# Moving a layer norm's roots off GpSimd: square roots on ScalarE, reciprocals and offsets on VectorE

## The chip, the cores and the metric

One core of one Trainium2 chip runs the whole program in one launch. The metric is device time in microseconds (us). A core has TensorE (PE; its weight loads are PEld), VectorE (DVE), ScalarE (ACT), GpSimd (POOL) and SyncE (SP), each with a queue of its own that it works off in order; they wait for each other through semaphores.

## The reference

Eight layers follow each other, each with a residual and a layer norm behind it. The change lies in the seventh, an attention over learned keys (4096 keys of 128, values of 128), on x of shape 4 x 1024 x 128:

```python
Q = jnp.einsum('bsd,bdr->bsr', x, shared_compress)
scores = jnp.einsum('bsr,nr->bsn', Q, K) / math.sqrt(K.shape[1])
topk_scores, topk_idx = jax.lax.top_k(scores, 8)
weights = jax.nn.softmax(topk_scores, axis=-1)
selected_V = V[topk_idx]
output = jnp.einsum('bskd,bsk->bsd', selected_V, weights)
...
r = x + output
x = (r - mean(r)) / jnp.sqrt(var(r) + 1e-5)
```

## The kernel before

The stage is `top_keys_stage`. A prelude works out `shared_compress`; after it the stage runs over 32 tiles of 128 tokens (ALL = 32), eight to a batch, in eight groups of four (PER_HALF = 4, GROUPS = 8). All of it is written out straight, with no hardware loop, and the order on each engine is that of the calls in its function. For tile t:

- TensorE multiplies the queries of the tile by all 4096 keys, in four chunks of 1024 columns (L2945), into two banks that ScalarE must empty by turns. Behind the chunks of tile t it mixes tile t - 6 (`mix`, L2931): eight products with the identity add the eight weighted values.
- ScalarE copies the chunks to `scores` (L2619), of which four tiles are kept. Between the second and the third chunk it weights the gathered values of tile t - 6 (`scale`, eight instructions, L2596), before the fourth it normalises tile t - 14 (`normalise`, L2606). Behind the last chunk comes `weigh` for tile t - 1: it waits for the eight best scores, negates the largest (L2585) and takes the exponentials (L2587). Behind the loop it works off what is left: `scale` up to tile 31, and `normalise` up to tile 31, one tile of each a turn.
- VectorE searches the eight best scores of tile t (`dve.max`, L2746) and their indices (L2748), then closes tile t - 5 (`close`): reciprocal of the sum of weights, r = mix * inverse + x (L2760), and mean and variance into `moments` (L2763, L2764). `close` waits for the mix of its tile.
- GpSimd gathers the values of tile t (`gather`): eight indirect DMAs (L2534), one for each of the eight indices; they wait for the indices of tile t and for the mix of tile t - 8, whose slot they use. `root(g)` stands behind `gather(4g + 8)`: it waits for the moments of the four tiles of group g, and then takes four operations of 128x4, among them (var + eps) to the power -0.5 (L2525, L240, L241, L2527). They give `rstd` and `offset` = -mean * rstd, by which `normalise` computes y = r * rstd + offset on ScalarE.
- SP stores y a group at a time (L2498, it waits for `normalise` of the group's last tile), loads x again for the groups to come (L2494), and behind the store of the group before the last fetches the first input of the next stage (`next_x`, L2506). The stage ends when the last stores have landed.

The next stage, `routed_experts_stage`, begins with a transpose of that input, and its first exponential on ScalarE is L3112.

## Time and profile before

| | us |
|---|---|
| median of three runs | 2123.44 (2122.04 to 2123.99) |
| profiled execution, its own time | 2122.32 |
| its span | 2120.4 |
| TensorE busy in the span | 1879.8 (89%) |
| VectorE busy | 1569.4 (74%) |
| ScalarE busy | 1227.2 (58%) |
| GpSimd busy | 610.6 (29%) |
| gathers of the stage (L2534), 256 | 242.3, mean 947 ns |
| root operations on GpSimd, 4 x 8 | 13.2 |

The stage with the gathers takes the span from about 1510 to 1977 us; its loop over tiles begins near 1608. The shares of busy time are means over stages with different limits, so they don't say what bounds this one; the timelines of the stage do. A timeline row gives the start and the length in us, engine, line, operation, output and inputs, and in square brackets how long the engine had stood idle before it and what ended that ("issue": nothing that the profile shows). Issue rows of SP and GpSimd are the issuing of a DMA, not the transfer.

### The profile page before, as it was taken

The numbers are of one execution on the slowest core, as the hardware profiler recorded it, in microseconds if no ns is written. First come the engines' busy times: TensorE is split into PE (matmuls) and PEld (weight loads), VectorE is DVE, ScalarE is ACT, GpSimd is POOL, SyncE is SP. The second block draws the span as 40 slices with busy tenths as digits, with TensorE's granted clock in tenths as the row PEclk, the third lists the DMA queues.
The fourth block names the chain that finished last, engine by engine and source line by source line (L and its number), as shares of the span: only waits on it lengthen the run. The fifth ranks groups of instructions, "written<-read, shape, count | busy, mean of one in ns | idle before, by whom it ended". The sixth has DMA issues, their size and how long they took to land. (4 is left out here: it accounts for less than half of the span.)

```text
span 2120.4 us, 31998 instructions
## 1 busy us (share of the span) xinstructions
PE 1879.8 (89%) x10615; PEld 1279.2 (60%) x10624; DVE 1569.4 (74%) x3770; ACT 1227.2 (58%) x2532; POOL 610.6 (29%) x801
## 2 busy tenths in 40 slices
PE   7999979999699999579999999999789989983797
PEld 5667644444477777458888887888664444443342
DVE  4555547677448888658999999999435999994498
ACT  3334436666255555178888887887214667673465
POOL 2221216778302121200000000000002777777122
PEclk9999989999699999789999999999779999996799
DMA  2000020000300000000000000000400122222100
GB/s 91 30 30 0 30 87 11 16 6 11 104 6 11 21 11 11 10 15 2 6 16 6 2 16 6 1 6 16 190 2 14 53 56 61 69 61 61 45 26 25
DMA packets 34695, 65.80 MB, mean 31 GB/s; under 512 B 8406, under 2 KB 19742, under 8 KB 33782
## 3 DMA queue, kind: packets, MB, share of 16 engines
q1 hardware_dynamic: 26358, 47.16, 6.5%
q0 software_dynamic: 8192, 16.79, 3.1%
q8 instruction: 80, 1.31, 0.3%
q14 instruction: 65, 0.53, 0.1%
HBM read 51.34 MB, written 12.58 MB: 30 GB/s over the span
## 5 line engine op out<-in xcount | busy, mean ns | idle before, releaser
L2183 DVE SCALAR_TENSOR_TENSOR pk_level<-pk_sums,pk_least 128x1024 f32<-128x1024 f32 x256 | 321.7, 1276 | 22.9 <-ACT pk_sums L2092 21.6
L2092 ACT ACTIVATE pk_sums<-pk_sum 128x512 f32<-128x512 f32 x512 | 278.7, 602 | 94.5 <-PE pk_sum L2302 92.1
L2534 POOL DMA_INDIRECT tk_values<-top_keys_values,tk_index x256 | 242.3, 947 | 196.4 <-DVE tk_index L2748 118.4
L2310 PE MATMUL pk_weights<-product_keys_early_ident,pk_level 128*128 128x128 f32 x2048 | 269.5, 274 | 26.3 <-DVE pk_level L2183 24.3
L2310 PEld LDWEIGHTS pk_weights<-product_keys_early_ident,pk_level 128*128 128x128 f32 x2048 | 225.9, 141 | 52.9 <-DVE pk_level L2183 33.8
L2945 PE MATMUL tk_to_act<-tk_keys,tk_xT 128*128 128x512 f32 x512 | 233.0, 602 | 23.2 <-ACT tk_scores L2619 22.1
L2945 PEld LDWEIGHTS tk_to_act<-tk_keys,tk_xT 128*128 128x128 f32 x512 | 94.1, 192 | 144.3 <-issue 92.5
L1755 PEld LDWEIGHTS er_outs<-experts_early_w,er_hT 128*128 128x128 f32 x1024 | 134.0, 192 | 59.7 <-issue 56.4
L1165 PE MATMUL ml_outs<-experts_early_we,ml_xT 128*128 128x512 f32 x320 | 161.3, 632 | 3.5 <-DVE ml_r L1022 3.5
L2302 PE MATMUL pk_sum<-pk_lay_corners,pk_partsT 96*128 96x256 bf16 x1024 | 154.2, 272 | 0.9 <-ACT pk_sums L2092 0.9
L2746 DVE MAX8 tk_best<-tk_scores 128x8 f32<-128x4096 f32 x32 | 141.1, 4409 | 15.1 <-ACT tk_scores L2619 15.1
L240 POOL TENSOR_TENSOR pk_plus_eps<-pk_moments,pk_eps 128x4 f32<-128x4 f32 x8 | 11.2, 1406 | 452.3 <-DVE pk_moments L224 452.3
L2748 DVE FIND_INDEX8 tk_index<-tk_best,tk_scores 128x8 uint32<-128x4096 f32 x32 | 141.4, 4419 | 0.0
L1022 DVE SCALAR_TENSOR_TENSOR ml_r<-ml_outs,ml_gates,ml_r 128x128 f32<-128x128 f32 x384 | 105.0, 342 | 47.7 <-PE ml_outs L1165 36.7
L1448 ACT ACTIVATE er_hT<-er_to_act,experts_early_b 128x512 f32<-128x512 f32 x128 | 85.5, 686 | 93.2 <-PE er_to_act L1744 92.3
L2619 ACT ACTIVATE tk_scores<-tk_to_act 128x1024 f32<-128x1024 f32 x128 | 126.2, 1011 | 20.4 <-PE tk_to_act L2945 20.4
L1755 PE MATMUL er_outs<-experts_early_w,er_hT 128*128 128x128 f32 x1024 | 134.5, 275 | 0.0
L1744 PE MATMUL er_to_act<-er_xT,experts_early_w 128*128 128x512 f32 x256 | 133.4, 604 | 0.0
L2073 ACT ACTIVATE pk_partsT<-pk_to_act 96x1024 bf16<-96x1024 bf16 x128 | 132.0, 1036 | 0.0
L2302 PEld LDWEIGHTS pk_sum<-pk_lay_corners,pk_partsT 96*128 96x128 bf16 x1024 | 99.6, 97 | 26.0 <-issue 15.4
L2931 PE MATMUL tk_to_dve<-tk_values,top_keys_early_ident 128*128 128x128 f32 x512 | 69.6, 295 | 38.6 <-ACT tk_values L2596 38.6
L891 ACT ACTIVATE ml_scaled<-ml_outs,ml_gates 128x128 f32<-128x128 f32 x256 | 70.1, 387 | 52.7 <-PE ml_outs L1165 51.6
(437 smaller groups left out, 3677.4 us busy)
## 6 DMA issues: line engine op xcount, KB each, us to landing
tk_scores<-top_keys_compress SPq DMA_DIRECT2D x1, 4096.0 KB
tk_values<-top_keys_values,tk_index POOLq DMA_INDIRECT x256, 2.5
att_x_proj<-x_first SPq DMA_DIRECT2D x4, 512.0 KB, 5.0
att_x_res<-x_first SPq DMA_DIRECT2D x4, 512.0 KB, 4.3
x_after_attention<-att_y SPq DMA_DIRECT2D x4, 512.0 KB, 4.9
experts_early_w<-experts_w SPq DMA_DIRECT2D x2, 1024.0 KB
x_after_attention<-ml_y SPq DMA_DIRECT2D x8, 256.0 KB, 2.0
experts_ahead_x<-x_after_attention SPq DMA_DIRECT2D x8, 256.0 KB, 3.3
```

The source lines that it names most:

```text
L1165: pe.matmul(outs[f % len(outs)][:], xT[:, b % 2, t * P:(t + 1) * P], we[:, n * PER_FILL:(n + 1) * PER_FILL, :].rearrange("p e d -> p (e d) ...
L1744: pe.matmul(bank[:], w1[:, n, :], xT[:, t % 2, :], start=True, stop=True).then_inc(A.full.sem, 1)
L1755: ins = pe.matmul(bank[:, s * P:(s + 1) * P], hT[:, (t * CHUNKS + n) % (LAG + 1), s * P:(s + 1) * P], w2[:, n, :], start=k == 0 and s == 0 ...
L2073: act.activation(partsT[:, t % 3, s * PER_FILL:(s + 1) * PER_FILL, :].rearrange("k n p -> k (n p)"), bank[:].bitcast(BF16)[0:STACK, 0:PER_ ...
L2092: act.activation(sums[:, n % SUMS, half * HALF:(half + 1) * HALF], bank[:], ACT.Copy).then_inc(S.free.sem, 1)
L2183: dve.scalar_tensor_tensor(level[:, n % LEVELS, :], sums[:, n % SUMS, :], least[:, t % 2, h:h + 1], sums[:, n % SUMS, :], ALU.is_ge, ALU.m ...
L2302: ins = pe.matmul(by_column[:, j], partsT[:, t % 3, h * FILLS + c, :], lay_corners[:, c], start=True, stop=True)
L2310: ins = pe.matmul(weights[:, ch * P:(ch + 1) * P], level[:, n % LEVELS, ch * P:(ch + 1) * P], ident[:], is_transpose=True, start=h == 0 an ...
L2534: pool.indirect_dma_start(out=values[:, slot, k, :], out_offset=None, in_=c["values"], in_offset=bass.IndirectOffsetOnAxis(ap=index[slot][ ...
L2746: dve.max(best[:, slot, :], scores[:, t % KEPT, :]).then_inc(best_ready, 1)
L2748: dve.max_index(index[slot][:], best[:, slot, :], scores[:, t % KEPT, :]).then_inc(index_ready, 1)
L2945: ins = pe.matmul(bank[:, half * HALF:(half + 1) * HALF], xT[:, b, at * P:(at + 1) * P], keys[:, first:first + HALF], start=True, stop=True)
```

## The change

The four root operations leave GpSimd. `deviate(g)` on ScalarE takes the square root of var + eps for the four tiles of group g; in the loop it stands behind the last chunk of tile 4g + 10 and ahead of `weigh`, and for groups 6 and 7 in the turns 34 and 38 behind the loop, ahead of `normalise` of that turn (tiles 20 and 24). `offset_of(g)` on VectorE takes the reciprocal and -mean * rstd; it stands behind the close of tile 4g + 5, and for the last group at the very end. GpSimd's queue then holds the gathers alone, and three of its constants go.

```diff
+    ROOT_LAG = 2 * PER_HALF + 2
...
-            pool.memset(power[:], -0.5).then_inc(built, 1)
             pool.memset(eps[:], LN_EPS).then_inc(built, 1)
-            pool.memset(minus_one[:], -1.0).then_inc(built, 1)
-            pool.wait_ge(built, 4)
-
-            def root(g):
-
-                group = half_of(g)
-                pool.wait_ge(moments_ready, (g + 1) * PER_HALF)
-                after(pool, offset_ready, g)
-                steps.do(pool.tensor_tensor(minus_mean[:], moments[:, group, 0], minus_one[:], ALU.mult))
-                steps.link(rsqrt_on_pool(steps, pool, rstd[:, group], moments[:, group, 1], plus_eps[:], eps[:], power[:]))
-                pool.tensor_tensor(offset[:, group], minus_mean[:], rstd[:, group], ALU.mult).then_inc(offset_ready, 1)
+            pool.wait_ge(built, 2)
...
-            for t in range(ALL + CLOSE_LAG):
-                if t < ALL:
-                    gather(t)
-                g, at = divmod(t - CLOSE_LAG, PER_HALF)
-                if g >= 0 and at == PER_HALF - 1:
-                    root(g)
+            for t in range(ALL):
+                gather(t)
...
+            def deviate(g):
+
+                group = half_of(g)
+                act.wait_ge(moments_ready, (g + 1) * PER_HALF)
+                act.activation(deviation[:, group], moments[:, group, 1], ACT.Sqrt, bias=eps[:]).then_inc(deviation_ready, 1)
...
+                if t >= ROOT_LAG and (t - ROOT_LAG) % PER_HALF == 0:
+                    deviate((t - ROOT_LAG) // PER_HALF)
                 if t >= 1:
                     weigh(t - 1)
...
+                if t >= ROOT_LAG and (t - ROOT_LAG) % PER_HALF == 0 and (t - ROOT_LAG) // PER_HALF < GROUPS:
+                    deviate((t - ROOT_LAG) // PER_HALF)
                 normalise(t - NORM_LAG)
...
+            def offset_of(g):
+
+                group = half_of(g)
+                dve.wait_ge(deviation_ready, g + 1)
+                after(dve, y_ready, (g - 1) * PER_HALF)
+                steps.link(dve.reciprocal(rstd[:, group], deviation[:, group]))
+                dve.scalar_tensor_tensor(offset[:, group], moments[:, group, 0], -1.0, rstd[:, group],
+                                         ALU.mult, ALU.mult).then_inc(offset_ready, 1)
...
                 if t >= CLOSE_LAG:
                     close(t - CLOSE_LAG)
+                    g, at = divmod(t - CLOSE_LAG, PER_HALF)
+                    if at == 1 and g >= 1:
+                        offset_of(g - 1)
...
+            offset_of(GROUPS - 1)
```

## Rows read from the trace of the kernel before

**Rows 1.** Source view and timeline of the gathers: ns min/median/max, range; then start, length

```profile
L2534 POOL DMA_INDIRECT tk_values<-top_keys_values,tk_index x256: 940/944/1209, 1628.5 to 1959.5; - x128
...
1628.50 1.21 POOL L2534 DMA_INDIRECT tk_values<-top_keys_values,tk_index  x1 [117.44 <-DVE tk_index L2748]
```

**Rows 2.** Timeline, GpSimd (POOL), around its sixth root and its last gather

```profile
1927.50 0.95 POOL L2534 DMA_INDIRECT tk_values<-top_keys_values,tk_index  x1 [0.30 <-issue]
...
1928.47 0.21 POOL L2525 TENSOR_TENSOR tk_minus_mean<-tk_moments,tk_minus_one 128x4 f32<-128x4 f32 x1
...
1930.73 1.02 POOL L2534 DMA_INDIRECT tk_values<-top_keys_values,tk_index  x1 [0.51 <-issue]
...
1932.06 0.94 POOL L2534 DMA_INDIRECT tk_values<-top_keys_values,tk_index  x1 [0.30 <-issue]
...
1959.51 0.94 POOL L2534 DMA_INDIRECT tk_values<-top_keys_values,tk_index  x1 [0.30 <-issue]
```

**Rows 3.** Timeline, VectorE (DVE): index searches of tiles 8 and 31

```profile
1697.03 4.42 DVE L2748 FIND_INDEX8 tk_index<-tk_best,tk_scores 128x8 uint32<-128x4096 f32 x1
...
1923.75 4.42 DVE L2748 FIND_INDEX8 tk_index<-tk_best,tk_scores 128x8 uint32<-128x4096 f32 x1
```

**Rows 4.** Timeline of one tile in the steady part, ScalarE (ACT) and TensorE (PE)

```profile
1801.50 1.01 ACT L2619 ACTIVATE tk_scores<-tk_to_act 128x1024 f32<-128x1024 f32 x1
...
1805.38 0.20 ACT L2585 ACTIVATE tk_minus<-tk_best 128x1 f32<-128x1 f32 x1 [2.87 <-DVE tk_best L2746]
...
1805.62 0.30 ACT L2587 ACTIVATE tk_weight<-tk_best,tk_minus 128x8 f32<-128x8 f32 x1
...
1806.97 3.70 PE L2945 MATMUL tk_to_act<-tk_keys,tk_xT 128*128 128x512 f32 x8 [0.92 <-ACT tk_scores L2619]
```

**Rows 5.** Timeline, ScalarE, table loads of an earlier stage

```profile
591.30 1.28 ACT L1452 ACT_TABLE_LOAD   x1
...
592.60 0.21 ACT L1452 ACTIVATE er_exps<-er_shifted 128x16 f32<-128x16 f32 x1
...
632.53 1.28 ACT L1470 ACT_TABLE_LOAD   x1
...
635.81 0.42 ACT L1470 ACTIVATE er_probs<-er_biased 128x256 f32<-128x256 f32 x1 [2.00 <-DVE er_biased L1600]
```

**Rows 6.** Groups of instructions: busy us, mean ns; a reciprocal of 128x4

```profile
L2725 DVE RECIPROCAL tk_neuron_sum<-tk_neuron_sum 128x4 f32<-128x4 f32 x1 | 0.2, 178 | 0.0
```

**Rows 7.** Timeline, end of the stage

```profile
1964.42 2.02 ACT L2606 ACTIVATE tk_y<-tk_r,tk_offset,tk_rstd 128x128 f32<-128x128 f32 x5
...
1964.92 1.86 SPq L2498 DMA_DIRECT2D x_after_top_keys<-tk_y  x2
...
1969.31 0.18 DVE L2764 BATCH_NORM_AGGREGATE tk_moments<-tk_stats 128x2 f32<-128x6 f32 x1
...
1971.31 1.65 ACT L2606 ACTIVATE tk_y<-tk_r,tk_offset,tk_rstd 128x128 f32<-128x128 f32 x4 [4.87 <-POOL tk_offset L2527]
...
1972.98 0.32 SPq L2498 DMA_DIRECT2D x_after_top_keys<-tk_y  x1
...
1977.73 0.10 POOL L3073 MEMSET moe_power<- 128x4 f32 x1 [6.45 <-POOLq L154]
```

**Rows 8.** DMA issues at the stage's end: count, KB each, us from issue to landing

```profile
x_after_top_keys<-tk_y SPq DMA_DIRECT2D x3, 256.0 KB, 2.0
...
experts_ahead_x<-x_after_top_keys SPq DMA_DIRECT2D x1, 512.0 KB, 3.5
```

**Rows 9.** Timeline, ScalarE, first exponential of the next stage

```profile
1984.16 0.22 ACT L3112 ACTIVATE moe_expo<-moe_gate_bank 128x64 f32<-128x64 f32 x1 [3.67 <-PE moe_gate_bank L3268]
```

**Rows 10.** Windows: length, busy us by engine, TensorE clock granted, DMA share, GB/s

```profile
1700.00:1800.00 100.00, 90.62 (x325) 48.12 (x324) 98.61 (x72) 69.30 (x162) 75.97 (x85) 1.00 0.22 59
...
856.30:858.96 2.66, 0.01 (x2) 0.01 (x1) 2.66 (x2) 0.00 (x0) 0.00 (x0) 1.00 0.00 0
...
863.82:866.00 2.18, 1.44 (x5) 0.92 (x6) 1.80 (x9) 1.47 (x2) 1.47 (x2) 0.74 0.00 0
```

More of the change, by code:

```diff
@@ L2395, in top_keys_stage @@
         ones = m.sb("ones", [P, P])
-        power = m.sb("power", [P, PER_HALF]); eps = m.sb("eps", [P, PER_HALF]); plus_eps = m.sb("plus_eps", [P, PER_HALF])
-        minus_one = m.sb("minus_one", [P, PER_HALF]); minus_mean = m.sb("minus_mean", [P, PER_HALF])
+        eps = m.sb("eps", [P, 1]); deviation = m.sb("deviation", [P, KEPT_R])
         x = first_x.x; xT = m.sb("xT", [P, B, T])
@@ L2444, in top_keys_stage @@
         gathered = [m.sem(f"gathered{i}") for i in range(SLOTS)]
-        r_ready, moments_ready, offset_ready, y_ready = (m.sem(n) for n in ("r_ready", "moments_ready", "offset_ready", "y_ready"))
+        r_ready, moments_ready, deviation_ready, offset_ready, y_ready = (
+            m.sem(n) for n in ("r_ready", "moments_ready", "deviation_ready", "offset_ready", "y_ready"))
         dve_steps, pool_steps = m.sem("dve_steps"), m.sem("pool_steps")
@@ L2885, in _ @@
             ins.then_inc(chain_full, 1)
-            pe.wait_ge(built, 4)
+            pe.wait_ge(built, 2)
             pe.wait_ge(chain_ready, 4)
```

## The prediction

> **What bounds the kernel now.** I read the views in this order: the page's list of groups, to find the stage (it runs from about 1510 to 1977 us of the span); the source view of the gathers; the timeline of each engine in the steady part; then the timeline of the stage's end. The question at each is who is never idle.
>
> GpSimd is. Its 256 gathers begin at 1628.50, after one wait of 117.44 us for the first index, and the last begins at 1959.51 [rows 1]. In an undisturbed stretch they start (1959.51 - 1932.06) / 22 = 1.248 us apart: about 0.94 of work and 0.30 of issue. Where a root stands between two gathers, the starts 1927.50 and 1932.06 are 4.56 us apart and not 2.50, so one root costs the queue 2.06 us [rows 2]. Of the eight roots six stand between gathers; in GpSimd's loop root(g) follows gather(4g + 8), and only g = 0 to 5 are followed by more gathers. The sum closes: 255 x 1.248 + 0.27 for the longer first gather + 6 x 2.06 = 330.8 us, against 331.0 measured [rows 1, 2]. So GpSimd waits for nobody after its start, and its queue alone sets the time of the last gather.
>
> VectorE is the close second. From tile 8 to tile 31 its index searches start (1923.75 - 1697.03) / 23 = 9.86 us apart [rows 3]; GpSimd needs 8 x 1.248 = 9.98 us a tile without roots. ScalarE has 2.87 us of every tile to spare, in which it waits for the best scores, and TensorE waits 0.92 us once a tile for a bank that ScalarE must empty [rows 4].
>
> **The roots leave GpSimd.** 6 x 2.06 = 12.4 us go out of the queue that sets the end. Root 6 and root 7 stand behind the last gather and belong to the tail, below. The last gather then starts at 1959.51 - 12.4 = 1947.1, if the index is there. What is late next? Index 8 is ready at 1697.03 + 4.42 = 1701.5, and gather 8 would start at 1628.8 + 64 x 1.248 = 1708.6: 7.2 us of reserve. Index 31 is ready at 1928.2, gather 31 would start at 1628.8 + 248 x 1.248 = 1938.3: 10.1 us [rows 1 to 3]. The reserve pays for what VectorE gets.
>
> **VectorE takes a reciprocal and a product per group.** Six of the eight offset_of calls come before the index of tile 31. A reciprocal of 128x4 took 0.18 us [rows 6]; a product of the same size I take alike, and two gaps of 0.04: 0.43 us each call, 2.6 us in all, from a reserve of 10.1. Between 0.36 (no gaps) and 1 us a call this costs nothing. It does not wait either: offset_of(g) stands after tile 4g + 10, and its deviation is made by ScalarE behind the scores of tile 4g + 10, a tile before VectorE searches that tile. If it did wait, the next max search would be queued behind it, and behind that the indices of all later gathers.
>
> **ScalarE takes eight square roots, and table loads with them.** The steady part has only copies, exponentials and identities, and no load. In an earlier stage, where Gelu and Exp alternate, each change shows a load of 1.28 us, and the activation starts 0.02 us behind it (591.30 + 1.28, then 592.60) [rows 5]. The load does not wait for the data of its activation: at 632.53 it runs at once, and the activation follows at 635.81 after 2.00 us of waiting for VectorE [rows 5]. In the loop deviate(g) stands between the last scores of a tile and weigh. The load for Sqrt and the root itself (0.21 us for an exponential of 128x16 [rows 5], 0.30 for one with a bias read from memory [rows 4]; I take 0.30) need 1.6 us and fall into the 2.87 us of waiting. The moments are two tiles old by then, so no wait is added. The load back to Exp falls behind minus, after the best scores have come: 1.3 us, six times, in which the scores of the next tile are not taken and TensorE waits 2.2 us instead of 0.92. TensorE works 90.62 of 100 us at full clock, 8.93 us a tile, so it wins back 0.92 us a tile, 3.7 us in a group of four [rows 4, 10]. ScalarE itself has 4 x 2.87 = 11.5 us a group for 2.9 us of additions. Cost: nothing, with TensorE's spare time as the cover; without it, up to 6 x 1.3 = 7.8 us.
>
> The Trainium skill speaks against this part. "ScalarE: Activation LUTs", section "What ACT_TABLE_LOAD costs", gives 2.66 us for a change of set, with a drain, and the section on table sets says to do all of one set before the other. By its figure, 13 changes would be an estimate of 35 us of ScalarE and not 17, but the sum would stay, since 5.6 us a group still fit in 11.5; the trace shows 1.28 and no gap for a drain [rows 5]. The figure would lengthen TensorE's stops to some 3.6 us, which bears on the last rival.
>
> **The next stage.** It starts with an exponential, and the set is now that of Sqrt. ScalarE stands idle 3.67 us before it [rows 9], and by rows 5 the load runs before the wait: nothing. If the load came behind the wait: 1.28 us on the way to the gates. I take nothing.
>
> **The tail.** The last moments come at 1969.31 + 0.18 = 1969.49. Now the root on GpSimd ends and ScalarE normalises the last four tiles from 1971.31 to 1972.96: 3.47 us behind the moments [rows 7]. The four tiles of group 6 were normalised at 1964.42 (five in 2.02 us) while the last tile was still in work [rows 7]. After the change deviate(7) stands before them in ScalarE's queue and waits for the last moments. So behind the moments come a hop of 0.03, the root 0.30, and eight tiles at 0.40 to 0.41: 3.6 us; VectorE's offset (0.43) is hidden behind the first four. That is 0.1 us worse (0 to 0.4). No second load is due there, since root 6 has left the set in place.
>
> Moved with these tiles are DMAs on SP's queue: the store of group 6, and behind it the fetch of the next stage's first input, both of which used to be issued before the last moments [rows 7]. They are now issued some 2.0 to 2.6 us behind the moments, and the last store at 3.6. The fetch takes 3.5 us to land and a store 2.0 [rows 8]. If the last store shares the engines with the fetch, it starts late: it lands at 5.6 undisturbed, and at 2.6 + 3.5 + 2.0 = 8.1 if all of it follows the fetch. Between 0 and 2.5 us; I take 1.1, since only its data and not its start-up has to follow. From the last store's issue to the next stage 1977.73 - 1972.98 = 4.75 us pass as before [rows 7].
>
> **The sum.** -12.4 + 0.1 + 1.1 = -11.2 us. The profiled execution took 2122.32 us (span 2120.4), so it would become 2111.1 (span 2109.2). The median of the three runs is 1.1 above the profiled one; on the median I forecast 2112. The bounds: -12.4 gives 2111.0; tail at its worst (+2.9), 2114; with 1.28 for the next stage's load, 2115.2. Medians spread by about 1 us.
>
> **Rivals.** (A) VectorE becomes the bound. It happens if an offset_of costs more than 10.1 / 6 = 1.7 us, say because it waits for ScalarE. At 2.87 us each, the length of ScalarE's own wait, index 31 comes at 1928.2 + 17.2 = 1945.4, 7.1 behind the queue: 2119. For it: VectorE has 98.61 us busy in 100 [rows 10], no spare time at all. Against it: the deviation is ready a tile ahead.
>
> (B) The tail costs far more: the late fetch and stores pile up by more than their landing times say, or the next stage's load is exposed too: 2116.
>
> (C) The change does not shorten the queue: what follows a root is not the root but something that the ring of gathers needs anyway, so that gathers stretch by what the roots free. Time 2123. Against it: 22 gathers in a row keep 1.248 us [rows 2], and the DMA engines are at 0.22 [rows 10].
>
> (D) Slower: TensorE's clock. The six stops of 2.2 us let the granted clock fall, and TensorE, which has 0.92 us of spare time a tile, becomes the bound. After a single stop of 2.66 us in an earlier stage the clock was still 1.00 (from 856.30), but in the stretch from 863.82, after a second stop close behind, 0.74 [rows 10]. If a whole tile then ran at half clock, a group would lose 8.9 + 1.3 - 3.7 = 6.5 us; six are 39 us. Two covers come off once. GpSimd's reserve of 10.1 less the 2.6 for VectorE is 7.5 us. The scores of a tile, done at 1801.50 + 1.01, are there 8.3 us before their max search: the search before ends at 1805.38, so theirs starts at 1805.38 + 9.86 - 4.42 = 1810.8 [rows 3, 4]. 39 - 15.8 - 11.2 = 12 us slower than before: 2135. It decides from a loss of (15.8 + 11.2) / 6 = 4.5 us a group; below that the kernel is still faster. Against it: one stop of 2.2 us in 39 us of work is less than what left the clock at 1.00. The stops of 3.6 us by the Trainium skill's figure would make it likelier.
>
> **Chances.** Forecast (2109.5 to 2115) 0.78; A 0.05; B 0.08; C 0.04; D 0.05. The range 2109 to 2117 takes in the forecast and B. A measurement of this kernel tells 0.2% (4.2 us) from no change: faster means below 2119.2. Forecast, B and half of A are faster: 0.89; C and the other half 0.06; slower is D, 0.05.
>
> **What would show it.** Right: GpSimd's line has only gathers, from about 1628.5 to 1947.1, always 1.248 apart; seven loads for Sqrt and six for Exp in ScalarE's lines, of 1.28 us, and one more in the next stage before its wait; TensorE's waits of 0.92 become 2.2 once a group and its clock stays at 1.00; MAX8 never waits for scores; the last three DMA issues of the stage lie within 2 us. Wrong: waits of gathers for tk_index (A), gathers longer than 1.248 apart (C), a clock below 1.00 between 1700 and 1900 (D), a stage whose end lies more than 10 us behind the last moments (B). The forecast also falls if the loads do not run ahead of waits.

## The result, and the profile after

The changed kernel took 2110.3 us (median of four runs, 2108.26 to 2111.31) against 2123.53 (2122.04 to 2123.99) for the kernel before on the same chip: a ratio of 0.9935, 95% interval 0.992 to 0.995. That is faster by 13.2 us; the forecast was 11.2 us less and 2112 for the median, with a range from 2109 to 2117. The profiled execution took 2110.27, its span is 2108.4.

The page of the changed kernel, span and busy time of each engine (share of the span, instructions):

```profile
span 2108.4 us, 32001 instructions
...
PE 1884.2 (89%) x10615; PEld 1281.7 (61%) x10624; DVE 1571.8 (75%) x3786; ACT 1249.2 (59%) x2554; POOL 597.4 (28%) x767
```

Busy shares have hardly moved. TensorE is busy a little longer than before (1884.2 against 1879.8) and the kernel is 12 us shorter. The page doesn't say where they went; the source view of the gathers, now line 2524, does (ns min/median/max, first and last start, then the idle time before them):

```profile
L2524 POOL DMA_INDIRECT tk_values<-top_keys_values,tk_index x256: 940/944/1212, 1631.2 to 1949.8; - x128
...
  DVE tk_index L2744: 119.4, 1
  issue: 76.8, 252
  PE tk_to_dve L2940: 0.9, 3
```

256 gathers now run from 1631.2 to 1949.8, 318.6 us, against 331.0 in [rows 1]. They wait for an index once, at the start. So the 12.4 us are gone and nothing has moved into their place. To find the rest, both spans were cut at the same events, all read from timelines. The differences add up to the -12.0 us of the spans:

| stretch of the span, us | before | after | difference |
|---|---|---|---|
| stages before this one | 1510.92 | 1511.83 | +0.91 |
| start of the stage to first gather | 117.58 | 119.41 | +1.83 |
| first gather to last gather | 331.01 | 318.59 | -12.42 |
| last gather to last moments | 9.98 | 10.00 | +0.02 |
| last moments to end of the last y | 3.47 | 3.40 | -0.07 |
| last y to issue of last store | 0.02 | 0.03 | +0.01 |
| issue of last store to next stage | 4.75 | 4.65 | -0.10 |
| the last stage | 142.68 | 140.46 | -2.22 |

The third row is the change. The second and the last are larger than any change of the tail, and were not in the forecast.

One group boundary in the steady part of the changed kernel, ScalarE and TensorE by the timeline; it answers to [rows 4]:

```profile
1786.15 1.28 ACT L2590 ACT_TABLE_LOAD   x1
1787.45 0.30 ACT L2590 ACTIVATE tk_deviation<-tk_moments,tk_eps 128x4 f32<-128x4 f32 x1
1789.00 0.20 ACT L2571 ACTIVATE tk_minus<-tk_best 128x1 f32<-128x1 f32 x1 [1.25 <-DVE tk_best L2742]
1789.22 1.28 ACT L2573 ACT_TABLE_LOAD   x1
1790.52 0.30 ACT L2573 ACTIVATE tk_weight<-tk_best,tk_minus 128x8 f32<-128x8 f32 x1
1791.87 5.40 PE L2954 MATMUL tk_to_act<-tk_keys,tk_xT 128*128 128x512 f32 x8 [2.21 <-ACT tk_scores L2611]
```

ScalarE loads its table at once and takes the root, all within what was an idle time of 2.87 us; 1.25 us of it are left before `minus`. Then comes the load back, after the best scores are there, and the exponential of `weigh` and the next copy of scores are 1.3 us later than they were. TensorE stops for 2.21 us instead of 0.92. Six stops of 2.21 us stand in the loop. Behind three of them the eight matmuls took 5.40 us and not 3.70. TensorE's timeline, then windows (length, busy us by engine, granted clock, DMA share, GB/s):

```profile
1712.42 5.40 PE L2954 MATMUL tk_to_act<-tk_keys,tk_xT 128*128 128x512 f32 x8 [2.21 <-ACT tk_scores L2611]
1752.10 3.70 PE L2954 MATMUL tk_to_act<-tk_keys,tk_xT 128*128 128x512 f32 x8 [2.21 <-ACT tk_scores L2611]
...
1710.00:1720.00 10.00, 7.79 (x27) 4.32 (x27) 9.86 (x8) 8.10 (x18) 7.55 (x8) 0.83 0.19 53
1750.00:1760.00 10.00, 7.90 (x31) 4.55 (x32) 9.86 (x8) 8.36 (x20) 7.54 (x8) 1.00 0.21 54
1790.00:1800.00 10.00, 8.13 (x27) 4.58 (x28) 9.86 (x8) 8.07 (x19) 7.54 (x8) 0.83 0.20 52
```

The windows behind the stops of 1712.42 and 1791.87 have a granted clock of 0.83 (part of them at the lower of its two levels, 1.2 GHz), the one behind 1752.10 has 1.00. VectorE, in its timeline, does what it was given, and its max searches wait for scores only once, before the first:

```profile
1923.42 0.16 DVE L2767 RECIPROCAL tk_rstd<-tk_deviation 128x4 f32<-128x4 f32 x1
1923.62 0.20 DVE L2768 SCALAR_TENSOR_TENSOR tk_offset<-tk_moments,tk_rstd 128x4 f32<-128x4 f32 x1
```

### The profile page after: what moved, and what is told of

The parts are those of the page before. It is cut to its first block and busy times, and to the rows that moved or that the text cites. A ratio compares the mean times of both kernels' runs of the same rounds, so it can differ in the third digit from the quotient of the medians.

```text
span 2108.4 us, 32001 instructions
## 1 busy us (share of the span) xinstructions
PE 1884.2 (89%) x10615; PEld 1281.7 (61%) x10624; DVE 1571.8 (75%) x3786; ACT 1249.2 (59%) x2554; POOL 597.4 (28%) x767
## 5 line engine op out<-in xcount | busy, mean ns | idle before, releaser
L2524 POOL DMA_INDIRECT tk_values<-top_keys_values,tk_index x256 | 241.8, 945 | 197.1 <-DVE tk_index L2744 119.4
L240 POOL TENSOR_TENSOR pk_plus_eps<-pk_moments,pk_eps 128x4 f32<-128x4 f32 x8 | 11.2, 1406 | 453.1 <-DVE pk_moments L224 453.1
L1165 PEld LDWEIGHTS ml_outs<-experts_early_we,ml_xT 128*128 128x128 f32 x320 | 59.7, 200 | 63.4 <-issue 51.9
```

Of the source, the lines that this page charges most:

```text
L1165: pe.matmul(outs[f % len(outs)][:], xT[:, b % 2, t * P:(t + 1) * P], we[:, n * PER_FILL:(n + 1) * PER_FILL, :].rearrange("p e d -> p (e d) ...
L2524: pool.indirect_dma_start(out=values[:, slot, k, :], out_offset=None, in_=c["values"], in_offset=bass.IndirectOffsetOnAxis(ap=index[slot][ ...
```

## The experiments

All are edits of the changed kernel but for "roots twice", an edit of the kernel before. A figure for the gathers is the start of the last less the start of the first. The theory: the roots' time in GpSimd's queue is the whole gain, and what was added to ScalarE and VectorE is hidden. The rivals are those of the prediction: VectorE as the bound (A), the tail (B), a queue that isn't shortened by the roots (C), TensorE's clock (D).

### No root at all, and each root twice

Two ends of the same scale. Without roots: `rstd` is set to one and `offset` to zero once, and `normalise` waits for the moments. The kernel leaves this stage's layer norm out; the same holds wherever "no roots" is said below.

```diff
+            pool.memset(rstd[:], 1.0).then_inc(built, 1)
+            pool.memset(offset[:], 0.0).then_inc(built, 1)
...
-                    deviate((t - ROOT_LAG) // PER_HALF)
+                    pass
...
-                        offset_of(g - 1)
...
-                    act.wait_ge(offset_ready, g + 1)
+                    act.wait_ge(moments_ready, (g + 1) * PER_HALF)
```

Roots twice, from the kernel before:

```diff
-                steps.do(pool.tensor_tensor(minus_mean[:], moments[:, group, 0], minus_one[:], ALU.mult))
-                steps.link(rsqrt_on_pool(steps, pool, rstd[:, group], moments[:, group, 1], plus_eps[:], eps[:], power[:]))
+                for again in range(2):
+                    steps.do(pool.tensor_tensor(minus_mean[:], moments[:, group, 0], minus_one[:], ALU.mult))
+                    steps.link(rsqrt_on_pool(steps, pool, rstd[:, group], moments[:, group, 1], plus_eps[:], eps[:], power[:]))
```

> The changed kernel without any root: no square root on ScalarE, no reciprocal or offset on VectorE; rstd and offset are constants 1 and 0, so the layer norm of this stage is left out (its means and variances are still taken). Theory (GpSimd's queue of gathers sets the end, and what ScalarE and VectorE got is hidden): from the first to the last gather 318.6 us, as in the changed kernel; the time falls by the tail alone, which no longer has root and offset behind the last moments: about 1.7 us less than the changed kernel, ratio to before 0.993. Rival (the square roots with their table loads, or VectorE's additions, hold something up that the 318.6 us contain): the gathers take several us less than 318.6, and the time falls by that much more.

> The kernel before with three of the four operations of each root taken twice on GpSimd (the first repeat took 1.55 us in the trace, 1928.47 to 1930.02). Theory (a root's own length is in the queue that sets the end): six roots between gathers and the last one behind them are each 1.55 us longer, so first to last gather 331.0 + 9.3 = 340.3 us, and the time rises by 10.9 us, ratio 1.005. Rival C (the ring of gathers needs the pause anyway): the second repeat costs less than half of that, or the gathers are still 331 us.

Measured: 2220.21 and 2232.18 us, beside 2223.5 for the kernel before on that chip; ratios 0.9985 (0.9964 to 1.0006) and 1.0036 (1.0021 to 1.0051). On this chip the kernel before itself was 100 us longer than the 2123.5 of the result. Neither theory nor rival was tested by these numbers: the gathers took 423.6 us without a root and 433.3 with roots taken twice, and waited for indices in both. What held them is told under "A TensorE that is held", below.

### The last group's root later, and the load back to Exp earlier

Both stood on the same chip as the two above. The first normalises group 6 before `deviate(7)` and so takes the fetch and the store of group 6 out from behind the last moments; the second draws the load back to Exp in front of the wait for the best scores.

```diff
-                if t >= ROOT_LAG and (t - ROOT_LAG) % PER_HALF == 0 and (t - ROOT_LAG) // PER_HALF < GROUPS:
-                    deviate((t - ROOT_LAG) // PER_HALF)
+                if t == 4 * PER_HALF + 2 + 4 * PER_HALF:
+                    deviate(GROUPS - 2)
+                if t == ALL + 10:
+                    deviate(GROUPS - 1)
```

```diff
                     deviate((t - ROOT_LAG) // PER_HALF)
+                    act.activation(spare[:, t:t + 1], eps[:], ACT.Exp)
```

> The changed kernel with the last square root moved behind the four tiles of group 6 in ScalarE's queue. Theory (in the tail the chain is last moments, root, offset, and then whatever of the normalisation is left): the last normalisation ends 2.3 us behind the last moments and not 3.4, and the time is 1.1 us below the changed kernel's, ratio to before 0.993. Rival (the last store or the fetch for the next stage sets the end of the stage, not ScalarE): no change against the changed kernel.

> The changed kernel with one exponential of a single column into a spare tile right behind each square root of the loop, so that the load back to the table of Exp runs while ScalarE waits for the best scores. Theory: TensorE's six stops of 2.2 us go back to about 1.2 us, its granted clock stays at 1.00 between 1700 and 1900 (in the changed kernel it fell behind three of the six stops), and the time is that of the changed kernel within 1 us, since GpSimd's queue sets the end. Rival D in small (the stops and falls of the clock do cost time): the time falls by 2 us or more against the changed kernel.

Measured: 2223.27 (0.9988, 0.9965 to 1.0011) and 2224.56 (1.0011, 0.9981 to 1.004), beside the same 2223.5. As totals they say nothing, for the same reason. The tail is cut at its events all the same: in the first, 2.41 us from the last moments to the last y (3.40 in the change) and 3.39 from the last store to the next stage (4.65). Both are taken up in a combined kernel below.

### The two ends again, on another chip

> The same kernel as in e1 (no root on any engine, constants in place of rstd and offset, so the layer norm of this stage is left out), since in e1's measurement all engines also stood idle for reasons outside of the program and the kernel before took 2223 us. Theory (GpSimd's queue sets the end; the additions to ScalarE and VectorE are hidden): 318.6 us from first to last gather, as in the changed kernel; ratio to before 0.993, about 1.7 us less than the changed kernel. Rival (the additions hold something up): clearly fewer than 318.6 us between the gathers.

> The same kernel as in e2 (three of four operations of each root twice on GpSimd), measured again for the same reason. Theory: each root between gathers is 1.55 us longer, first to last gather 340.3 us, time up by 10.9 us, ratio 1.005. Rival C (the ring of gathers needs the pause anyway): less than half of that.

Measured: 2231.41 and 2231.59 us beside 2232.26; ratios 1.0013 (0.9987 to 1.004) and 1.0013 (0.999 to 1.0035). Here, too, the kernel before was some 109 us longer than in the result, and roots taken away or doubled made no difference. This is worth a look, since it is just what rival C would have given: a queue that roots do not lengthen.

**A TensorE that is held.** The source view of the gathers without roots has these rows:

```profile
L2526 POOL DMA_INDIRECT tk_values<-top_keys_values,tk_index x256: 942/947/1212, 1631.1 to 2073.5; - x128
  DVE tk_index L2747: 247.5, 18
```

119.2 of the 247.5 us are the wait for the first index; the other 128.3 are 17 waits in the middle. So here GpSimd is not the bound at all. Who is? TensorE's and ScalarE's timelines at one of the stalls (start, length, engine, ..., idle before and its releaser):

```profile
1775.17 3.60 PE L2954 MATMUL tk_to_act<-tk_keys,tk_xT 128*128 128x512 f32 x8
1785.64 1.22 PE L2954 MATMUL tk_to_act<-tk_keys,tk_xT 128*128 128x512 f32 x1 [6.88 <-ACT tk_scores L2614]
```

```profile
1784.57 1.02 ACT L2614 ACTIVATE tk_scores<-tk_to_act 128x1024 f32<-128x1024 f32 x1 [9.00 <-remote]
```

The eight matmuls are modelled to end at 1778.77. ScalarE, whose next work is to copy the bank of scores that they filled, starts at 1784.57, after 9.00 us of idling that the profile puts down to "remote", since no instruction of this core ends where the semaphore rises. ScalarE had 19 such waits, 100 us, between 1640 and 1960. So what TensorE hands on came late, in bursts: here 5.8 us behind the modelled end. The longest single wait of this kind was 9.5 us in that stretch, and 21.0 us in the first trace of the roots taken twice. Whether its matmuls really ended later or only their signals came late, and by what, the trace does not show. It was so with either kernel, and was gone from one of the two chips later (the last three runs below stood on it). Its cause is open. What it means for the reading is plain: in that condition GpSimd waits for indices, and taking the roots away altogether is worth next to nothing (0.9985 and 1.0013).

### The change itself, on a third chip

> The changed kernel as it is, beside the kernel before. In the runs e1 to e7 the kernel before took 2223 to 2232 us, and the semaphore updates of TensorE in the stage came up to 20 us behind the modelled ends of its matmuls, so TensorE was held by something outside of the program. Theory: where TensorE is held, it and not GpSimd's queue is what the stage waits for, GpSimd waits for indices, and the change brings nothing: ratio 0.998 to 1.002, first to last gather about as long as before. Where it is not held (kernel before near 2123 us), 318.6 us between first and last gather and a ratio of 0.993 to 0.995. Rival: the 12.4 us of the roots are gained in both conditions, ratio 0.994 also beside a kernel before of 2225 us.

Measured: 2108.85 us beside 2125.59, ratio 0.9919 (0.9903 to 0.9936). Gathers 318.59 us, the tail 3.41 and 4.66, six stops of 2.21 us in TensorE, and the same three of them followed by slow matmuls as in the first trace. The result repeats on a chip without the holding; the ratio lies a little below the expected 0.993 to 0.995, which its interval just reaches. This kernel itself was never run on a chip with the holding, so the other half of the expectation stays untested; only edits of it and of the kernel before were.

### Roots twice and the two edits together, undisturbed

The combined kernel has both edits shown above.

> The kernel of e2 (three of four operations of each root twice on GpSimd), once more, for a chip on which TensorE is not held. Theory (a root's length lies in the queue that sets the end): each root between gathers 1.55 us longer, first to last gather 340.3 us, time up by 10.9 us, ratio 1.005. Rival C (the ring of gathers needs the pause anyway): less than half of that.

> The changed kernel with both edits of e3 and e5: the last square root stands behind the four tiles of group 6, and one exponential of a single column into a spare tile follows each square root of the loop. Where TensorE is not held (kernel before near 2125 us). Theory: the end of the stage is set by GpSimd's queue and, behind it, by moments, root, offset and four tiles of normalisation: 318.6 us from first to last gather, no stop of TensorE of 2.2 us between 1700 and 1900 and a granted clock of 1.00 there, last normalisation 2.3 us behind the last moments instead of 3.4; 1.1 us below the changed kernel in all, ratio to before 0.9915. Rival 1 (stops and falls of the clock cost time): 3 us or more below the changed kernel. Rival 2 (the end of the stage waits for the last store and the fetch, not for ScalarE): no gain.

Measured: roots twice 2139.15 us beside 2125.01, ratio 1.0054 (1.0037 to 1.007); both edits 2109.29, ratio 0.992 (0.9904 to 0.9937). GpSimd's timeline with the roots taken twice:

```profile
1760.67 0.94 POOL L2535 DMA_INDIRECT tk_values<-top_keys_values,tk_index  x1 [0.30 <-issue]
1761.63 0.21 POOL L2526 TENSOR_TENSOR tk_minus_mean<-tk_moments,tk_minus_one 128x4 f32<-128x4 f32 x1
...
1763.19 0.20 POOL L2526 TENSOR_TENSOR tk_minus_mean<-tk_moments,tk_minus_one 128x4 f32<-128x4 f32 x1
...
1766.75 0.94 POOL L2535 DMA_INDIRECT tk_values<-top_keys_values,tk_index  x1 [0.30 <-issue]
```

The two gathers around the root start 1766.75 - 1760.67 = 6.08 us apart, against 4.56 in [rows 2]: a repetition costs 1.52 us, six of them 9.1. The gathers took 340.11 us, 9.1 more than the 331.01. What stands in GpSimd's queue between two gathers comes out one for one at the last gather, and rival C falls. The kernel was slower by more than these 9.1 (14.1 us by the medians; 17.1 by the spans of the two profiled executions, which were not measured side by side): 1.5 more in the tail (4.98 us from moments to y), and the last stage took 149.47 us for 142.68, on which more below.

With both edits TensorE's waits for ScalarE between 1700 and 1900 are 0.78 to 1.22 us, none of them 2.2, and its clock is 1.00 from 1700 to 1900. The gathers took 318.85 us, as without the edits. So the stops and the slow matmuls behind them cost the change nothing. The tail did get shorter, by ScalarE's and SP's timelines:

```profile
1960.03 0.30 ACT L2591 ACTIVATE tk_deviation<-tk_moments,tk_eps 128x4 f32<-128x4 f32 x1 [3.08 <-DVE tk_moments L2764]
1960.77 1.65 ACT L2599 ACTIVATE tk_y<-tk_r,tk_offset,tk_rstd 128x128 f32<-128x128 f32 x4 [0.44 <-DVE tk_offset L2772]
```

```profile
1957.52 0.32 SPq L2507 DMA_DIRECT2D experts_ahead_x<-x_after_top_keys  x1
1962.43 0.32 SPq L2499 DMA_DIRECT2D x_after_top_keys<-tk_y  x1
1965.81 0.80 SPq L3067 DMA_DIRECT2D moe_x<-x_after_top_keys  x2
```

The fetch is now issued 2.5 us ahead of the last moments and 4.9 ahead of the last store, and lands before that store is issued: 3.38 us from the last store to the next stage, and only four tiles stand behind the root, 2.42 us from moments to y. Together that is 5.8 us, 2.25 less than in the change. The kernel as a whole was not faster by them (0.992, where the change itself had 0.9919): its last stage took 142.81 us and the change's 140.46.

### No roots, every tile a change of table, and a dear offset, undisturbed

The second edit makes ScalarE change its table to Sqrt and back in every tile, not in every fourth; the third takes the reciprocal 21 times, some 4 us more each `offset_of`.

```diff
                     deviate((t - ROOT_LAG) // PER_HALF)
+                elif t >= ROOT_LAG:
+                    act.activation(spare[:, t:t + 1], eps[:], ACT.Sqrt)
```

```diff
-                steps.link(dve.reciprocal(rstd[:, group], deviation[:, group]))
+                for again in range(21):
+                    steps.link(dve.reciprocal(rstd[:, group], deviation[:, group]))
```

> The kernel of e1 (no root on any engine, constants in place of rstd and offset, so the layer norm of this stage is left out), for a chip on which TensorE is not held. Theory (what ScalarE and VectorE got is hidden under the gathers): 318.6 us from first to last gather, as in the changed kernel. Behind the last moments four normalisations alone, 1.7 us, and from the issue of the last store to the next stage 3.4 us as in e9, so the stage is 3.0 us shorter than in the changed kernel; with the last stage at 140 to 143 us the time is 2105 to 2108, ratio 0.991 to 0.993. Rival (the additions hold something up): the gathers take clearly less than 318.6 us.

> The changed kernel with a square root of one column into a spare tile in each of tiles 11 to 31 that has no deviate, so that ScalarE changes its table to Sqrt and back in every tile (22 changes there and back, not 6). Theory of the prediction (TensorE's spare time is the cover, and each load back to Exp stops it for 2.2 us): with 8.9 us of work, a stop of 2.2 and a clock that falls behind half of the stops (1.7 us each), a tile takes 12.0 us and not 9.98; 22 tiles less 15.8 us of covers are 28 us more than the changed kernel, ratio to before 1.006. Rival (the stops heal themselves: once TensorE lags, its banks are empty while ScalarE loads, and only ScalarE's own 9.9 us a tile count): less than 6 us more than the changed kernel.

> The changed kernel with the reciprocal of each offset_of taken 21 times, which adds 20 x 0.20 = 4.0 us to each of the eight calls on VectorE. Theory (GpSimd has a reserve of 10.1 us before it waits for an index, of which 2 us are spent): six calls bring the last index 24 us later, 16 us behind the queue, so about 16 us more from first to last gather (334 or 335 us), and 4 us in the tail: 20 us more than the changed kernel, ratio to before 1.003; gathers start waiting for indices from about the second or third call on. Rival (VectorE has its own slack, or GpSimd follows VectorE anyway): no waits of gathers and no change, or the full 24 us and more.

Measured, beside 2122.41 us for the kernel before:

| kernel | us | ratio (95%) | gathers | moments to y | store to next stage | last stage |
|---|---|---|---|---|---|---|
| no roots | 2104.94 | 0.9919 (0.99 to 0.9939) | 318.59 | 1.68 | 3.39 | 140.38 |
| table changed in every tile | 2108.7 | 0.9931 (0.9911 to 0.9951) | 318.60 | 3.41 | 5.07 | 140.42 |
| offset 4 us dearer | 2135.41 | 1.0057 (1.0039 to 1.0074) | 335.87 | 6.67 | 3.39 | 147.62 |

**No roots.** With no root on any engine the gathers take as long as in the change, to 0.01 us:

```profile
L2526 POOL DMA_INDIRECT tk_values<-top_keys_values,tk_index x256: 940/944/1212, 1623.9 to 1942.5; - x128
```

So the additions to ScalarE and VectorE are hidden wholly. Against the change, only the tail has something left: 1.7 us less from moments to y and 1.3 less behind the store. The ratio, 0.9919, is that of the change on the third chip.

**A change of table in every tile.** This is the run that surprised: the theory's 28 us more did not come, and the rival's "less than 6 us" is what was measured. 22 loads for Exp and 23 for Sqrt stand in the loop and its tail, and the gathers take 318.60 us. TensorE stops for 2.21 us once, at the first of the changes (1711.19), and from there on it waits 0.92 to 1.22 us a tile, near the 0.92 of [rows 4]. ScalarE's timeline shows why:

```profile
1796.03 1.28 ACT L2616 ACT_TABLE_LOAD   x1
1797.32 0.20 ACT L2616 ACTIVATE tk_spare<-tk_eps 128x1 f32<-128x1 f32 x1
1797.60 0.20 ACT L2572 ACTIVATE tk_minus<-tk_best 128x1 f32<-128x1 f32 x1
1797.82 1.28 ACT L2574 ACT_TABLE_LOAD   x1
```

`minus` at 1797.60 does not wait any more. The first change makes ScalarE later, from then on its whole turn lies later, and both loads fall into what used to be its wait for the best scores. The 2 x 1.28 + 0.20 = 2.8 us that a tile now adds (2.9 in every fourth, which has the real root) just fill the 2.87 us of [rows 4]. The window shows how near that is to the end: ScalarE is busy 95.41 of 100 us, against some 78 in the change.

```profile
1700.00:1800.00 100.00, 89.21 (x320) 47.45 (x320) 98.55 (x75) 95.41 (x187) 75.48 (x80) 1.00 0.23 61
```

A delay that recurs in every turn shifts the schedule once, and no more, as long as it fits the idle time of the engine that carries it. In the change it comes in one turn of four; that the schedule falls back in between, and TensorE therefore stops again each time, is how I read the six equal stops. The next stage began 5.07 us behind the issue of the last store and not 4.65. All of that lies in the landing of the store, 3.71 us behind its issue against 3.29 in the change; from landing to next stage it is 1.36 us in both. Why it landed later is open.

"ScalarE: Activation LUTs" of the Trainium skill, section "Table sets: the hidden batching unit", advises doing all of one set before the other. No run here lost time by not doing so: the extra 16 changes and back cost the gathers nothing, since they fitted into ScalarE's spare time. What more would have cost was not run.

**A dear offset.** GpSimd's waits for an index, by its timeline:

```profile
1782.44 0.94 POOL L2524 DMA_INDIRECT tk_values<-top_keys_values,tk_index  x1 [1.45 <-DVE tk_index L2744]
...
1826.47 0.94 POOL L2524 DMA_INDIRECT tk_values<-top_keys_values,tk_index  x1 [4.40 <-DVE tk_index L2744]
...
1958.38 0.94 POOL L2524 DMA_INDIRECT tk_values<-top_keys_values,tk_index  x1 [4.29 <-DVE tk_index L2744]
```

From the index search of tile 8 to that of tile 31 VectorE now takes 253.9 us and not 226.7 [rows 3]: 4.53 us for each of six calls. The first is paid by the reserve, the second uses it up (the wait of 1.45 us at 1782.44 has 0.30 of issue in it, as every gather has), and each of the four that follow is paid nearly in full: 4.0 to 4.1 us beyond the issue (VectorE wins back 0.12 us a tile, as GpSimd needs 9.98 and VectorE 9.86). 1.15 + 4.10 + 4.00 + 4.09 + 3.99 = 17.3 us, which is just what the gathers took more than in the change (335.87 - 318.59). Reckoned from the reserve: 6 x 4.53 - 10.1 = 17.1. This is rival A made to happen, and VectorE's reserve is what the prediction said it was. The ratio is above the expected 1.003. Beyond the gathers, the slowdown lies in the tail (3.3 us more to the last y, since the last group's offset is in it) and in the last stage.

## Why the prediction was right

**The roots out of the queue: -12.4 predicted, -12.42 measured.** Right in size and in cause. 6 x 2.06 came from [rows 2]; the last gather was forecast 318.6 us after the first and is. That rival C would not do was argued from 22 gathers at an even pace; shown it is by the roots taken twice.

**VectorE: nothing.** Right. The two instructions of a call are 0.16 and 0.20 us long (1923.42 and 1923.62 above) and fill 0.40 us with the gap between them; reckoned were 0.43, and no max search waited for the deviation: the root that ended at 1787.75 was used at 1804.3. The index searches of tiles 8 to 31 take 1.8 us longer than before, 0.30 for each of six calls. Rival A falls for this kernel. That it begins at about 1.7 us a call was reckoned and not run; the dear offset, at 4.53, bears out the reserve that it was reckoned from.

**ScalarE and TensorE: nothing, for a reason that was half right.** The loads were as forecast to the hundredth: seven for Sqrt, six back to Exp, 1283 ns each, ahead of the wait the first, behind it the second; By the Trainium skill ("ScalarE: Activation LUTs", section "What ACT_TABLE_LOAD costs") the load is about 1283 ns, and a drain of about 1380 ns makes it 2.66 us. The load agrees to the nanosecond. For the drain there is no room: the load at 1786.15 began 0.01 us after the copy ahead of it had ended, and the root began 0.02 us behind the load. TensorE's 2.21 us were forecast as 2.2. But "TensorE's spare time as the cover" would have had a change in every tile lose time, since 1.3 us a tile is more than 0.92. It lost none. The cover is ScalarE's idle time, in steady state, not TensorE's. So the term was rightly put at nothing, but by the wrong account.

**Rival D happened in small.** The prediction held one stop of 2.2 us in 39 us to be too little for the clock to fall. It fell to 0.83 over 10 us behind three of six such stops, at 1.7 us of loss each. That step of the prediction was wrong. The other three stops, and the one in the run with a change in every tile, were just as long and left 1.00, so the length of the stop alone does not decide it; what does is open. The point from which it would decide, 4.5 us a group, was not reached, and the losses came back: a stop's extra 1.3 and these 1.7 are less than the 3.7 us that TensorE has to spare in four tiles [rows 4]. The kernel without such stops has the same gathers within 0.3 us (318.85).

**The next stage's load: nothing.** Right. It ran at 1970.69, and its exponential at 1974.34 had still waited 2.37 us for TensorE (3.67 in [rows 9]):

```profile
1959.65 0.18 DVE L2760 BATCH_NORM_AGGREGATE tk_moments<-tk_stats 128x2 f32<-128x6 f32 x1
1959.86 0.30 ACT L2590 ACTIVATE tk_deviation<-tk_moments,tk_eps 128x4 f32<-128x4 f32 x1 [4.61 <-DVE tk_moments L2760]
1960.07 3.17 ACT L2598 ACTIVATE tk_y<-tk_r,tk_offset,tk_rstd 128x128 f32<-128x128 f32 x8
...
1962.15 0.36 SPq L2507 DMA_DIRECT2D experts_ahead_x<-x_after_top_keys  x1
1963.26 0.32 SPq L2499 DMA_DIRECT2D x_after_top_keys<-tk_y  x1
...
1967.91 0.10 POOL L3082 MEMSET moe_power<- 128x4 f32 x1 [17.13 <-POOLq L154]
...
1970.69 1.28 ACT L3121 ACT_TABLE_LOAD   x1
...
1974.34 0.22 ACT L3121 ACTIVATE moe_expo<-moe_gate_bank 128x64 f32<-128x64 f32 x1 [2.37 <-PE moe_gate_bank L3277]
```

**The tail: +1.2 predicted, about -0.1 measured. This is the step that failed: a term was missing.** The timeline above is its end in the changed kernel. From the last moments to the last y it is 3.40 us for 3.6: a hop, the root and eight tiles, as described; the tiles begin before the root has quite ended. The fetch is issued at 1962.15 and the last store at 1963.26, 1.1 us apart, and the store landed 3.29 us after its issue against 2.03 before: 1.26 for the forecast 1.1 of pile-up. Right, too. What was wrong is "from the last store's issue to the next stage 4.75 us pass as before". That time was taken as a constant; it has parts, and one of them belonged to GpSimd. SP's waits at the end of the stage before (us in total, times, longest), and the drain of GpSimd in the source view of that barrier:

```profile
SPq L2509 <- DMA x_after_top_keys<-tk_y: 1.7, 1, 1.7
SPq L2388 <- PEq L2388: 1.5, 1, 1.5
```

```profile
L2388 POOLq DRAIN  x1: 5557/5557/5557, 1971.0 to 1971.0; - x1
```

And after:

```profile
SPq L2510 <- DMA x_after_top_keys<-tk_y: 3.0, 1, 3.0
SPq L2389 <- PEq L2389: 0.2, 1, 0.2
```

```profile
L2389 POOLq DRAIN  x1: 20262/20262/20262, 1935.8 to 1935.8; - x1
```

Before, the last store landed at 1975.01, and SP then waited another 1.5 us for the barrier. The view names TensorE's queue for it, but GpSimd was last: by the source view the drains of TensorE, VectorE and ScalarE had ended by 1973.0, and GpSimd's, begun at 1971.04 with the last operation of the last root, took 5.56 us and ended at 1976.60. After, GpSimd's last work is the last gather, which ends at 1950.8; its drain ends at 1956.1, and the barrier waits 0.2. In all fourteen traces this drain ends 5.30 to 5.33 us behind GpSimd's last instruction of the stage, whatever that was. So the +1.26 of the pile-up and some -1.36 of the drain stand in the same 4.65 us. The runs separate the two. Roots twice: the 1.5 us of barrier are there as in the kernel before, 4.75 us in all. Both edits: root off GpSimd but no pile-up, 3.38 us, so the drain alone is 1.37. The change: pile-up on top of that, 4.65, so the pile-up alone is 1.27. The root's real price in the tail of before was thus 1.4 us higher than [rows 7] seemed to say.

**What was not forecast at all: +0.9, +1.8 and -2.2 us outside the gathers and the tail.** The stages before this one and the prelude are the same code. Over the eight undisturbed traces the stretch from the stage's start to the first gather took 117.6 us in four (before, no roots, roots twice, table changed in every tile) and 119.4 in four (the change in both its traces, both edits, dear offset). It goes with TensorE's granted clock and not with an edit: over the 20 us that begin 70 us into the stage it was 0.90 in the kernel before and 0.84 in the change, and all eight traces fall into these two patterns. The last stage took 140.4 to 140.5 us in four of them, 142.7 and 142.8 in two and 147.6 and 149.5 in two. Windows of 20 us that begin 20 us into the last stage: the kernel before, the change, and roots twice:

```profile
1997.70:2017.70 20.00, 19.38 (x73) 7.56 (x74) 15.79 (x42) 10.97 (x20) 2.34 (x3) 0.91 0.00 1
```

```profile
1987.90:2007.90 20.00, 19.38 (x86) 7.75 (x85) 16.29 (x43) 12.60 (x24) 3.02 (x3) 1.00 0.00 1
```

```profile
2008.10:2028.10 20.00, 19.74 (x58) 8.74 (x57) 10.80 (x29) 7.30 (x15) 0.00 (x0) 0.57 0.00 0
```

TensorE was busy over 19 of 20 us in each, and was granted 0.91, 1.00 and, in the third, 0.57: mostly the lower of its levels. The length follows the clock in all eight: 1.00 in the four of 140.4 to 140.5 us, 0.91 in the two of 142.7 and 142.8, 0.57 and 0.58 in the two longest. These two are the ones that began latest (near 1988), but the start is not the reason: in the six traces with the holding the last stage began between 2065 and 2088 and took 140.0 to 140.6 us. What sets the clock there stays open.

Of the -12.04 us of the spans, -12.42 are the gathers, -0.14 all that lies between the last gather and the next stage, and +0.52 these three together. Against the forecast of -11.2 the tail is 1.34 us better and the three are 0.52 worse. That the three nearly cancel is luck: they were not in the forecast, and a last stage as slow as the two slowest, 7 to 9 us above the fastest, would have hidden half of the gain and more. What the forecast can claim is the row of the gathers. The 2.25 us that the two edits won in the tail were lost in the same way: 2.35 more in the last stage.

## What to carry to other kernels

Read the engine whose queue never idles, count what stands in it between the pieces of work that set the pace, and move that to engines with idle time in the same turn: the gain here was the count times the duration, to 0.1 us in 12. Compare two kernels stretch by stretch, between the same events: here a granted clock that changed from one execution to the next moved the total by 2 us in one stage and up to 9 in another, without any link to the edits. Test the cover by steady state: a delay that recurs every turn only shifts the schedule, so it counts against the idle time of the engine that carries it, and not against the next engine's. And a constant between the last transfer and the next stage is a maximum over all engines at a barrier; list who is last there before calling it unchanged.

## What the runs showed of the hardware

- GpSimd's drain at the end of this stage ended 5.30 to 5.33 us behind its last instruction in all fourteen traces, whether that was a root (1971.28 to 1976.60 before) or a gather (1950.78 to 1956.08 after; the drain's record begins there before the last gathers, so only its end can be used). VectorE's took 0.11 us in the same barrier.
- Eight matmuls took 5.40 us for 3.70 behind three of six stops of 2.21 us, in two traces at the same three places; the granted clock of 10 us around them was 0.83. Behind the other three, just as long, it was 1.00.
- A table load took 1283 ns in every one of the cases. Where its activation had to wait, it ran ahead of the wait (1970.69 for 1974.34); 45 in a stage cost the gathers nothing.
- The last stage, the same code in every kernel, took 140.4, 142.7 or 147.6 to 149.5 us at granted clocks of 1.00, 0.91 and 0.57 to 0.58 in its second 20 us.
- On two chips what TensorE hands to ScalarE came late from about 1650 us on, in edits of either kernel. Single waits of ScalarE for it were up to 21.0 us long, 100 to 109 us were added to the whole, and no instruction in the traces accounts for it.
